# Softmax of a graph attention layer: dividing the mixed nodes instead of the probabilities, with the node products spread over the loop

## The reference

```
D[b,i,j,:] = |h[b,i,:] - h[b,j,:]|                  # for all pairs of nodes
s = leaky(batchnorm(D @ W1.T + b1)) @ W2.T + b2     # one score for each pair; batchnorm over all pairs
A = softmax over j of (s where adj > 0, else -9e15)
y = A @ h @ Wg.T + bg                               # attention
y = leaky(batchnorm(y) * gg + beg)                  # batchnorm over all graphs and nodes
x = x + concat(h, y) @ Wt.T + bt
```

## Time and profile before

| | us |
|---|---|
| median of 3 runs | 1128.88 |
| lowest and highest run | 1128.56, 1129.87 |
| time of the profiled execution | 1126.25 |
| its span from first to last instruction | 1124.3 |
| PE busy in the span | 1049.5 (93%) |
| DVE busy | 1033.1 (92%) |
| ACT busy | 1001.0 (89%) |
| POOL busy | 567.6 (50%) |
| pass 2, from the first L674 to the last scores | 661 to 998 |

### The profile page before, as it was taken

How to read it: one execution, slowest core, us unless ns; L and a number is a source line. 1 busy time by engine, 2 the same in 40 slices (tenths; PEclk the granted TensorE clock), 3 DMA queues, 4 the chain that set the end, 5 groups by cost and what they waited for, 6 DMA issues and landing times.

```text
span 1124.3 us, 17526 instructions
## 1 busy us (share of the span) xinstructions
PE 1049.5 (93%) x6390; PEld 461.6 (41%) x6390; DVE 1033.1 (92%) x1381; ACT 1001.0 (89%) x1268; POOL 567.6 (50%) x331
## 2 busy tenths in 40 slices
PE   3899999999999899999999989999999999978997
PEld 1333333333333333333333444233333333357786
DVE  5899999999999999999999985899999999948897
ACT  3889898999999899999999978999999999934897
POOL 5687678778777877777787700111121122201430
PEclk9999999999999999999999999999999999989999
DMA  6345443454444344454444487999999999960012
GB/s 183 139 153 196 159 175 153 168 198 168 194 171 179 140 186 180 168 196 169 185 182 178 179 327 269 337 361 329 334 347 326 342 332 329 324 175 14 20 58 76
DMA packets 99060, 233.31 MB, mean 208 GB/s; under 512 B 9120, under 2 KB 46464, under 8 KB 98976
## 3 DMA queue, kind: packets, MB, share of 16 engines
q1 hardware_dynamic: 86704, 219.97, 53.5%
q0 software_dynamic: 2240, 7.34, 1.8%
q10 hardware_dynamic: 10032, 4.89, 1.7%
HBM read 124.43 MB, written 107.74 MB: 206 GB/s over the span
## 4 chain that ended last, share of the span: by engine, by line
PE 50%; DVE 23%; ACT 14%; issue 9%; POOL 3%; ACTq 1%; DMA 0%; DVEq 0%; POOLq 0%
PE psum L789 21%; PE psum L799 10%; ACT store L674 8%; DVE store L294 8%; PE psum L803 8%; DVE plain_st L1099 3%; PE psum L902 3%; ACT store L593 2%; POOL store L294 1%; PE psum L779 1%; PE psum L761 1%; DVE store L1131 1%; PE psum L877 1%; ACTq L678 1%; DVE bst L1283 1%
## 5 line engine op out<-in xcount | busy, mean ns | idle before, releaser
L294 POOL TENSOR_TENSOR store<-h_ext 128x2048 f32<-128x2048 f32 (+1 forms) x96 | 386.3, 4025 | 95.7 <-PE psum L789 95.7
L789 PE MATMUL psum<-store,w1tt_sb 128*64 128x512 f32 x1792 | 422.8, 598 | 10.9 <-ACT store L593 10.8
L294 DVE TENSOR_TENSOR store<-psum,h_ext 128x2048 f32<-128x2048 f32 x160 | 363.9, 2274 | 0.6 <-ACT h_ext L563 0.6
L593 ACT ACTIVATE store<-store 128x2048 f32<-128x2048 f32 x160 | 305.7, 1928 | 19.3 <-DVE store L294 11.8
L674 ACT ACTIVATE store<-store,st 128x1024 f32<-128x1024 f32 x192 | 227.9, 1240 | 0.0
L789 PEld LDWEIGHTS psum<-store,w1tt_sb 128*64 128x64 f32 x1792 | 122.6, 136 | 249.5 <-issue 214.4
L799 PE MATMUL psum<-store,w_twice 128*64 128x512 f32 x768 | 201.6, 602 | 5.4 <-DVE store L294 2.9
L294 DVE TENSOR_TENSOR store<-h_ext 128x2048 f32<-128x2048 f32 x64 | 146.1, 2283 | 16.3 <-PE psum L789 16.0
L1099 DVE BATCH_NORM_STATS2 plain_st<-store 128x6 f32<-128x512 f32 x256 | 160.5, 678 | 0.0
L803 PE MATMUL psum<-early 128*64 128x512 bf16 x1152 | 159.0, 382 | 0.0
L605 ACT COPY store<-psum 128x1024 f32<-128x1024 f32 x128 | 128.4, 1024 | 16.7 <-PE psum L789 11.6
(11 more groups left out here) (161 smaller groups left out, 1088.4 us busy)
## 6 DMA issues: line engine op xcount, KB each, us to landing
kept_products<-store SPq DMA_DIRECT2D x192, 512.0 KB, 2.9
store<-kept_products SPq DMA_DIRECT2D x192, 512.0 KB, 5.8
early<-score_skew POOLq DMA_DIRECT2D x14, 384.0 KB, 6.8
early<-adj SPq DMA_DIRECT2D x16, 256.0 KB, 3.5
early<-adj_t SPq DMA_DIRECT2D x16, 256.0 KB, 3.6
store<-x ACTq DMA_DIRECT2D x16, 256.0 KB, 5.3
out<-early SPq DMA_DIRECT2D x16, 256.0 KB, 2.3
score_skew<-early POOLq DMA_DIRECT2D x14, 128.0 KB, 6.1
```

What stands on the lines that cost most here:

```text
L294: return engine.tensor_tensor(t[:, :, 0:steps, :], nodes.unsqueeze(2).broadcast_to([C, 2, steps, N]), windows(h_ext[:, 2 * c, :], STEP * m ...
L593: nc.scalar.activation(t, t, ACT.Abs).then_inc(abs_ready, 1)
L789: last = nc.tensor.matmul(t[MID * g:MID * g + MID, b, :], w1tt_sb[:, 0:MID], diff[slot][:, g, b * BANK:b * BANK + BANK], start=True, stop= ...
```

## The change

1. The exponentials are no longer divided. ACT takes the exponential in place (`s_shift`), PE transposes it as it is (TURN_E 47), DVE copies it out (COPY 48). At MIX 50 PE first multiplies the turned exponentials with a matrix of ones (one f32 matmul of 512 columns into `att[1]`), which leaves each row sum in every partition, and then mixes the nodes as before. NORM is gone. DVE takes the reciprocal of that bank, 128x512 elements, and multiplies the mixed nodes in `att[0]` with it on their way to `h_nat` (`att_divide`, Y 51). ACT's copy with the bias (L682) is gone; bg is taken into the second batchnorm's numbers instead, by two small DVE operations ahead of the wait for POOL, and one fewer behind it.
2. The mask is added by PE: `none_of(j)` on POOL makes a bf16 copy of the quad's `no_edge`, and SUM starts with one bf16 matmul of 512 columns with -9e15 times the identity. Of the eight f32 matmuls four are left (the transposed half); DVE adds the half that is not transposed when it takes the sum out of PSUM (`tensor_tensor` in place of L1225). The reload of `s_half` waits for `s_masked` in place of `s_sum`.
3. The 14 node products are spread: `weighted_nodes(u)` at n = 16 (u - 2) + 14 on PE and `nodes_out(u)` at n = 16 (u - 2) + 17 on ACT, all in bank 4.
4. The last part of the first split goes from POOL to DVE (at n = 1 of pass 1).
5. Y_SUMS goes to step 56; some of the folds of x get other places.

```
-        EVAC, DIST_T, TURN, SUM, SCORES, EXP, NORM, TURN_P, COPY, MIX, Y, Y_SUMS = 24, 25, 27, 41, 43, 45, 48, 49, 51, 53, 56, 57
+        EVAC, DIST_T, TURN, SUM, SCORES, EXP, TURN_E, COPY, MIX, Y, Y_SUMS = 24, 25, 27, 41, 43, 45, 47, 48, 50, 51, 56
+        WEIGHED, WEIGHED_OUT = 14, 17
-            return psum[:, 4 + u % 2, :].rearrange("p (b n) -> p b n", b=QUAD)
+            return psum[:, 4 + (u == 1), :].rearrange("p (b n) -> p b n", b=QUAD)
-        def mix_at(n):
-            u, r = divmod(2 * n, 3)
-            return EARLY_MIX + u if r < 2 and 0 <= u < NQ - EARLY_MIX else None
+        def mix_at(n, step):
+            u, r = divmod(n - step, QCH)
+            return EARLY_MIX + u if r == 0 and 0 <= u < NQ - EARLY_MIX else None
...
+            def none_of(j):
+                if j >= 2:
+                    pool.wait_ge(s_sum, j - 1)
+                nc.gpsimd.tensor_scalar(none[:, j % 2, :].rearrange("p (b n) -> p b n", b=QUAD), no_edge[0][:, quad(j), :],
+                                        1.0, None, ALU.mult).then_inc(none_set, 1)
...
-            def y_to_nodes(j):
-                act.wait_ge(out_mm, j + 1)
-                nc.scalar.activation(h_nat[:, quad(j), :], att[0], ACT.Identity, bias=BG).then_inc(y_out, 1)
...
-                nc.scalar.activation(prob[:, :, :], s_shift[:, :, :], ACT.Exp).then_inc(exp_done, 1)
+                nc.scalar.activation(s_shift[:, :, :], s_shift[:, :, :], ACT.Exp).then_inc(exp_done, 1)
...
-                for b in range(QUAD):
-                    nc.tensor.matmul(att[0][:, b, :], ident[:, :], s_half[:, b, 0:N], start=True, stop=False)
-                    last = nc.tensor.matmul(att[0][:, b, :], s_half[:, b, 0:N], ident[:, :], start=False, stop=True)
+                nc.tensor.matmul(att[0], neg_ident[:, :], none[:, j % 2, :], start=True, stop=False)
+                for b in range(QUAD):
+                    last = nc.tensor.matmul(att[0][:, b, :], s_half[:, b, 0:N], ident[:, :], start=False, stop=(b == QUAD - 1))
...
             def att_mix(j):
-                pe.wait_ge(prob_tr_ready, j + 1)
+
+                pe.wait_ge(exp_tr_ready, j + 1)
+                nc.tensor.matmul(att[1], ones[:, :], exp_tr[:, :, :], start=True, stop=True).then_inc(exp_summed, 1)
                 at_zero(QCH * j + MIX)
...
-                nc.vector.scalar_tensor_tensor(s_shift[:, :, :], no_edge[0][:, quad(j), :], NEG, att[0], ALU.mult, ALU.add)\
+                nc.vector.tensor_tensor(s_shift[:, :, :], att[0], s_half[:, :, 0:N], ALU.add)\
                   .then_inc(s_masked, 1)
...
-            def att_norm(j):
-                dve.wait_ge(exp_done, j + 1)
-                linked(nc.vector.tensor_reduce(rows[:, 1, :], prob[:, :, :], AX.X, ALU.add))
-                linked(nc.vector.reciprocal(rows[:, 2, :], rows[:, 1, :]))
-                nc.vector.tensor_tensor(prob[:, :, :], prob[:, :, :], bcast(rows[:, 2, :], N), ALU.mult)\
-                  .then_inc(prob_ready, 1)
...
+            def att_divide(j):
+                dve.wait_ge(exp_summed, j + 1)
+                nc.vector.reciprocal(sum_recip[:, :, :], att[1]).then_inc(recip_ready, 1)
+                dve.wait_ge(recip_ready, j + 1)
+                dve.wait_ge(out_mm, j + 1)
+                nc.vector.tensor_tensor(h_nat[:, quad(j), :], att[0], sum_recip[:, :, :], ALU.mult).then_inc(y_out, 1)
...
+                if n == 1:
+                    dve.wait_ge(y_mid, 1)
+                    nc.vector.tensor_tensor(y_part(0, 2), by_couple(y_rest[:, :]), y_part(0, 1), ALU.subtract).then_inc(y_split, 1)
```

More of the change, by code:

```diff
@@ L157, in two_layers @@
         s_shift = by_graph(late(1536, 512))
[L158 to L159 removed]
+        sum_recip = by_graph(late(2048, 512))
+        exp_tr = by_graph(late(2560, 512))
         adj_sb = [by_graph(late(3584 + 512 * t, 512).bitcast(I32)) for t in range(2)]
@@ L176, in two_layers @@
         soft = sb("soft", [128, 4, 3, QUAD])
+        none = sb("none", [128, 2, BANK], BF16)
+        neg_ident = sb("neg_ident", [128, 128], BF16)
         psum = ctx.enter_context(nc.psum_tensor("psum", [128, 8, BANK], F32))
@@ L212, in two_layers @@
         skew_cleared = [sem("skew_cleared0"), sem("skew_cleared1")]
-        s_sum, s_masked, dve_att, s_shifted, exp_done, prob_ready, prob_turned, prob_tr_ready, out_mm, y_ready = (
-            sem(n) for n in ("s_sum", "s_masked", "dve_att", "s_shifted", "exp_done", "prob_ready", "prob_turned",
-                             "prob_tr_ready", "out_mm", "y_ready"))
+        s_sum, s_masked, dve_att, s_shifted, exp_done, recip_ready, exp_turned, exp_tr_ready, out_mm, y_ready = (
+            sem(n) for n in ("s_sum", "s_masked", "dve_att", "s_shifted", "exp_done", "recip_ready", "exp_turned",
+                             "exp_tr_ready", "out_mm", "y_ready"))
         x_out, x_folded = sem("x_out"), sem("x_folded")
+        exp_summed = sem("exp_summed")
+        none_set, neg_set = sem("none_set"), sem("neg_set")
         weighted, weighted_ready, y_out = sem("weighted"), sem("weighted_ready"), sem("y_out")
@@ L324, in so_far @@
             return min(max(-((step - n) // QCH), 0), NQ)
-        FOLD_AT = [QCH * (NQ - 1) + TURN] * 2 + [QCH * (NQ - 2) + step for step in (SCORES + 1, NORM, COPY, Y_SUMS)] + \
-            [QCH * (NQ - 1) + step for step in (SCORES, NORM, COPY, COPY, COPY)]
+        FOLD_AT = [QCH * (NQ - 1) + TURN] * 2 + [QCH * (NQ - 2) + step for step in (SCORES + 1, COPY, Y, Y_SUMS)] + \
+            [QCH * (NQ - 1) + step for step in (SCORES, SCORES, COPY, COPY, COPY)]
         MADE_AT = (257, 258, 266, 267, 270, 273, 277, 282, 284, 285, 286)
@@ L478, in low @@
                   .then_inc(y_split, 1)
-            low(0)
             for n in range(CHUNKS):
@@ L526, in mask_l1 @@
                 nc.gpsimd.tensor_scalar(MASK[j % MRING], no_edge[1][:, quad(j), :], NEG, None, ALU.mult).then_inc(mask_set, 1)
+            nc.gpsimd.tensor_scalar(neg_ident[:, :], ident[:, :], NEG, None, ALU.mult).then_inc(neg_set, 1)
             for j in range(NQ):
+                none_of(j)
                 if j < BY_POOL:
@@ L698, in _ @@
                         load_x(q)
-                if mix_at(n) is not None:
-                    nodes_out(mix_at(n))
-                for step, do in ((Y, y_to_nodes), (EXP, exps)):
+                if mix_at(n, WEIGHED_OUT) is not None:
+                    nodes_out(mix_at(n, WEIGHED_OUT))
+                for step, do in ((EXP, exps),):
                     j = quad_at(n, step)
@@ L913, in at_one @@
             def at_one(n):
-                pe.wait_ge(weighted_ready, NQ)
-                for s, step in ((turn_ready, TURN), (prob_tr_ready, COPY)):
+                pe.wait_ge(weighted_ready, EARLY_MIX)
+                for s, step in ((turn_ready, TURN), (exp_tr_ready, COPY), (recip_ready, Y)):
                     if so_far(step, n) > 0:
@@ L952, in _ @@
                     products_again(n + LEAD_PROD)
-                if mix_at(n) is not None:
-                    weighted_nodes(mix_at(n))
+                if mix_at(n, WEIGHED) is not None:
+                    weighted_nodes(mix_at(n, WEIGHED))
                 m = n - LAG_SCORE
@@ L959, in _ @@
                     outputs_of_x(MADE_AT.index(n))
-                for step, do in ((DIST_T, turn_dist), (SUM, att_sum), (TURN_P, att_turn), (MIX, att_mix)):
+                for step, do in ((DIST_T, turn_dist), (SUM, att_sum), (TURN_E, att_turn), (MIX, att_mix)):
                     j = quad_at(n, step)
@@ L1256, in _ @@
                 for step, do in ((Y_SUMS, y_sums), (EVAC, take_rows), (TURN, take_turned), (SCORES, att_scores),
-                                 (NORM, att_norm), (COPY, att_copy)):
+                                 (COPY, att_copy), (Y, att_divide)):
                     j = quad_at(n, step)
@@ L1268, in _ @@
             nc.vector.tensor_scalar(bag[:, 2:3], bag[:, 1:2], EPS, None, ALU.add).then_inc(bn2_var, 1)
+            chain(bn2, nc.vector.tensor_tensor(bag[:, 0:1], bag[:, 0:1], BG, ALU.add))
+            chain(bn2, nc.vector.tensor_tensor(bag[:, 0:1], BG, bag[:, 0:1], ALU.subtract))
             dve.wait_ge(bn2_rstd, 1)
             chain(bn2, nc.vector.tensor_tensor(bag[:, 4:5], bag[:, 3:4], GG, ALU.mult))
-            chain(bn2, nc.vector.tensor_tensor(bag[:, 5:6], bag[:, 0:1], bag[:, 4:5], ALU.mult))
-            nc.vector.tensor_tensor(bag[:, 6:7], BEG, bag[:, 5:6], ALU.subtract).then_inc(bn2_ready, 1)
+            nc.vector.scalar_tensor_tensor(bag[:, 6:7], bag[:, 0:1], bag[:, 4:5], BEG, ALU.mult, ALU.add).then_inc(bn2_ready, 1)
             done[0] = 0
```

31 lines of the change are left out of this document (18 added, 13 removed).

## The result

The changed kernel takes 1173.53 us (median of 4 runs, 1172.41 to 1174.52) against 1129.08 for the kernel before in the same rounds: a ratio of 1.0389, interval 1.0372 to 1.0405. It is slower, by 44.4 us. The forecast was 1155 with a range to 1171, so the sign was right and the size was not. The profiled execution took 1174.33 us (span 1172.5), 48.1 more than the one of before. Its mean granted clock is 0.976, where it was 0.995.

A forecast was written before the change was run, and what follows sets the result against it. DVE was taken to set the pace before the change. Terms of -10.5 (start of pass 2), +35.8 (cycles), +2.5 (behind pass 2) and -1.5 (start of pass 1) gave +26.3 us: 1152.5 profiled, median 1155, range 1138 to 1171.

The forecast's parts named there:

- The start of pass 1: First chunks of pass 1: POOL's differences no longer wait behind the first split's last part, 1.5 us less.
- The start of pass 2: First chunks of pass 2: most node products leave them, so ACT needs less time; 10.5 us less.
- R: DVE's reciprocal of 128x512 in each quad: taken as 3.5 us, with ends 2.7 and 4.4.
- The second rival: DVE's reciprocal costs eight passes for a column, 4.4 us each, giving 1168.5 us; chance 0.2.
- The period: Later quads of pass 2: a loop through PE and DVE takes 23.2 us, DVE alone 22.5; 23.1 taken.
- ACT (19.1) and PE (20.7) wait inside it: Later quads of pass 2: both engines' work in us fits within the 23.1 us period.
- PE waiting at DIST_T for EVAC: Later quads of pass 2: a sign expected in the trace, along with periods of 23 us.
- Behind pass 2: Attention of the last quads up to the aggregate: 2.5 us more, with ends 0 and 5.
- net 1.4: Quad 13: its reciprocal and multiply ahead of EVAC 15 add 4.2 us, less ACT's copy that is gone.
- Behind the aggregate: From the aggregate to the kernel's end: a change of 0 us was forecast.
- The third rival: Start of pass 2: faster first chunks wait for loads, so the 10.5 us vanish, giving 1165; chance 0.06.
- The first rival: DVE's reciprocal is one pass of 0.68 us, PE sets the pace at 20.7, giving 1118.5, faster; chance 0.12.

The follow-up runs named there:

- e4_spread: The kernel before with only the 14 node products spread as in the change: 1123.71 us, ratio 0.9946 to the kernel before.
- e5: The changed kernel with the old division restored, all other parts kept: 1119.93 us, 0.9924 of the kernel before; run again on another chip, 1121.33 us, 0.9925.
- e2_fill: The changed kernel with eight unused bf16 matmuls filling PE's wait ahead of DIST_T: 1163.87 us, ratio 1.0299 to the kernel before.
- e1_copy: The changed kernel with the 128x512 reciprocal replaced by a copy, so nothing is divided: 1131.44 us, ratio 1.0013 to the kernel before.

## Why the prediction had the sign and the loop right, and the size wrong

- *The start of pass 1:* -1.7 for -1.5. *The start of pass 2:* -8.6 for -10.5. PE's first products there ran at 1.2 GHz behind a wait of 0.9 for DVE (3.68 us at 664.65 for a row that takes 1.94), which had been no part of the estimate. Up to EVAC 0 the clock is 0.83, before it was 0.95, and ACT waits 2.0 us for products. EVAC 0 of e4_spread comes 9.0 us earlier, with the same 3.68.
- *R:* 3.35 for 3.5, from a difference of 28 ns in rows of four and one columns. That it came so near is in part luck: 4 ns more or less of fixed time move R by 0.5 us. The second rival (4.4) fell by this.
- *The period:* the loop gave 23.2, "I take 23.1", and the six undisturbed cycles took 23.11. DVE's own load in them is 22.1. The agreement to 0.01 is luck: R was 0.15 shorter than in the sum, the wait at COPY 0.16 longer, and SUM is put at 1.2 there where its own two terms give 1.3. The first cycle took 1.5 more, with ACT full; e5, with the same start and the old division, has no such excess (20.05), so the start alone does not make it, and what does is open.
- *The step that failed* is "ACT (19.1) and PE (20.7) wait inside it". That put the cost of PE's wait at nothing. The wait is 2.2 to 2.9 us ahead of DIST_T in the 13 cycles, in six of them the granted clock fell at its end, and DIST_T, SUM and what follows ran at half rate inside the very loop that sets the pace: 10.3 us, shown by e2_fill. The prediction even named "PE waiting at DIST_T for EVAC" as a sign of being right. With the 1.5 of the first cycle this is nearly all of the 12.0 us missing in the row of 13 cycles.
- *Behind pass 2* +8.5 for +2.5. The term "net 1.4" for quad 13 was mis-sized; the 2.8 that it takes off the 4.2 rest on no row. ACT's copy of quad 13, taken off as a gain, was needed before only by Y_SUMS and not by EVAC 15; after, PE's outputs of x, the ones matmul, the reciprocal and the multiply all stand ahead of EVAC 15. Timeline of PE and DVE after in that stretch:

```profile
1035.03 1.91 PE L869 MATMUL psum<-wt_sb,h_ext 128*128 128x128 f32 x8
...
1038.57 1.02 PE L961 MATMUL psum<-early,ones 128*128 128x512 f32 x2
...
1039.63 3.36 DVE L1259 RECIPROCAL early<-psum 128x512 f32<-128x512 f32 x1 [10.37 <-PE psum L961]
```

  DVE stands 10.37 us until the row sums are there, then divides for 3.36, and EVAC 15 starts at 1044.36. The copy of before had waited 7.78 us behind ACT's DMA issues; that DVE's multiply has taken over the place in the order, the prediction did not see. That this is the cause is read from the trace; no run tried it by itself. From EVAC 14 to EVAC 15 e1_copy took 21.65 us and e5 18.84, so of the 6.4 that the changed kernel has more than e5 3.6 hang on the reciprocal's length.
- *Behind the aggregate* +2.3 for 0: the clock from 1072.6 to 1088.6 is 0.89, before in the stretch that answers to it 1.00. In the rest it is 0.97 for 0.99, and PE is busy 73.7 us there for 71.5. This is not the change's alone: the same kernel took 97.6 us behind the aggregate in e5_all_but_division and 99.2 in e5_again, both with 1.00 in these first 16 us and with 0.99 and 0.97 in the rest. What starts it is open. Windows of after and, below it, of before:

```profile
1072.60:1088.60 16.00, 11.99 (x79) 10.84 (x80) 13.05 (x51) 10.87 (x19) 3.25 (x4) 0.89 0.00 0
```
```profile
1026.70:1042.70 16.00, 12.56 (x100) 11.38 (x98) 12.90 (x50) 10.71 (x19) 3.90 (x4) 1.00 0.00 0
```

- *The third rival* (loads) fell: the start of pass 2 gave 8.6 of the 10.5, and no engine waits for a load there. But it was near: the DMA engines are full in that stretch (share 1.03), where before they had 0.85. View: the stretch of after up to EVAC 0 (columns as above).

```profile
659.31:688.60 29.29, 25.68 (x142) 6.72 (x144) 25.36 (x19) 27.32 (x26) 1.42 (x1) 0.83 1.03 407
```

- *The first rival* (a reciprocal in one pass) fell by its row, and e1_copy shows that its price was wrong too.

Twelve of the 21.8 us missing are in the cycles, 6.0 between EVAC 14 and the aggregate, 2.3 behind it and 1.6 at the starts.

## What to carry to other kernels

An operation that costs nothing on four columns can cost five copies on 512: before moving a division from sums to data, multiply its price per column by the new width. When another engine becomes the bound, PE's new wait is not free if it lies in the loop that sets the pace: check the granted clock behind it, and move matmuls that are off the loop into the wait (12 us here, by two numbers). Take such a change apart: two of its five parts alone, spread node products and one subtraction on another engine, were a gain of 0.7% hidden under a loss of 4.7%.

## What the runs showed of the hardware

- The DVE reciprocal of 128 x n f32: 351, 695, 895, 1695 and 3350 ns for n = 32, 96, 128, 256 and 512. A copy of 512 takes 683 to 692.
- In the kernel after, the granted clock fell to half around the end of a wait of 2.23 to 2.85 us in six cycles, and didn't in others with a wait of 2.24 to 2.88: the length of the one wait alone did not decide it. In four of the six it fell 0.2 to 0.8 us before DIST_T started, in the other two 0.4 us after.
- POOL's and DVE's instructions take longer where they overlap. Timeline of DVE and POOL in e5_all_but_division:

```profile
868.59 2.80 DVE L297 TENSOR_TENSOR store<-h_ext 128x2048 f32<-128x2048 f32 x1
869.32 4.08 POOL L532 TENSOR_SCALAR plain_st<-no_edge 128x512 f32<-128x512 uint8 x1
871.42 1.52 DVE L1148 TENSOR_SCALAR store<-store 128x2048 int32<-128x2048 int32 x1
```

  In other places of the same trace these take 2.28, 1.49 (POOL's at its shortest) and 1.23 us. The Trainium skill, "SBUF — State Buffer", section "Who interferes with whom", says that a DVE instruction with two SBUF inputs contends with a GpSimd instruction that reads SBUF, and that the shared ports are an exclusive lock: who starts first has them for the whole instruction and the other blocks. The trace agrees that they contend; but here the instruction that had started first was longer too (2.80), and the third ran to its end while POOL's was under way, so the rows show both sides stretched rather than one blocked (POOL's times in a profile are rough).
